# State update and layer-norm sums in two f16 parts; diagonal blocks of keys and state placed by DMA

## The reference

```
x = x + 0.5 * ffn(layernorm(x))
x = x + attn(layernorm(x))
x = x + 0.5 * ffn(layernorm(x))

ffn:  h = silu(x W1 * s1) * (x W2 * s2);  h = gelu(h H1 * t1);  h = gelu(h H2 * t2);  h W3 * s3
      (1024 hidden features, all weights in {-1, 0, 1})
attn: q, k, v, beta = split(layernorm(x) Wqkvb + b);  beta = sigmoid(beta);  k = k / |k| per head
      for every token t, per head (16 heads of 16 features):
          S = S + outer(beta_t * (v_t - S k_t), k_t);   o_t = S q_t
      x + o Wout + b
```

## Time and profile before

| | |
|---|---|
| median of 3 executions | 1703.59 us |
| profiled execution, own time | 1703.29 us |
| its span, first to last instruction | 1701.5 us |
| granted TensorE clock, mean | 0.998 |
| busy: PE / PEld | 97% / 60% |
| busy: DVE / ACT / POOL | 74% / 74% / 75% |

### The profile page before, as it was taken

The page is one execution under the profiler, slowest core; times in us unless marked ns, Lnnn a source line. Parts: engine busy times, 40 slices in busy tenths (PEclk is TensorE's granted clock), DMA queues, the critical chain, the costliest instruction groups (busy, mean ns, idle before and its releaser), DMA issues.

```text
span 1701.5 us, 31307 instructions
## 1 busy us (share of the span) xinstructions
PE 1651.6 (97%) x10385; PEld 1016.2 (60%) x10385; DVE 1258.3 (74%) x3152; ACT 1251.0 (74%) x2510; POOL 1279.5 (75%) x1594
## 2 busy tenths in 40 slices
PE   6989999999999999999999999999999999999999
PEld 5765556565656555565656565555656565655578
DVE  5456787878788787878787887878787878878541
ACT  4668687777778686887777786867877777867654
POOL 4574887969686877869696868778696868687563
PEclk9999999999999999999999999999999999999999
DMA  7200000000000000000000000000000000000000
GB/s 279 75 1 1 1 2 1 2 1 1 1 26 1 1 1 1 26 1 2 1 26 1 2 1 1 1 1 26 1 1 1 2 1 14 1 3 12 13 2 13
DMA packets 5279, 23.26 MB, mean 14 GB/s; under 512 B 640, under 2 KB 1664, under 8 KB 3584
## 3 DMA queue, kind: packets, MB, share of 16 engines
q1 hardware_dynamic: 5120, 21.26, 3.4%
HBM read 17.06 MB, written 4.19 MB: 12 GB/s over the span
## 4 chain that ended last, share of the span: by engine, by line
PE 60%; DVE 12%; POOL 8%; ACT 6%; issue 5%; DVEq 0%; POOLq 0%; ACTq 0%
PE ffn_bank L1152 37%; PE att_bank L1173 6%; PE ffn_bank L1135 5%; PE state_bank L1211 3%; POOL hid_lo L600 3%; POOL pairs L629 2%; DVE terms L998 2%; PE att_bank L1188 2%; PE att_bank L1189 2%; PE att_bank L1220 2%; ACT state_parts L783 2%; PE att_bank L1103 2%; DVE state_bank L1000 2%; DVE roots L875 1%; POOL pairs_lo L637 1%
## 5 line engine op out<-in xcount | busy, mean ns | idle before, releaser
L1152 PE MATMUL ffn_bank<-hid_hi,w_sb 128*128 128x448 f16 (+1 forms) x2880 | 941.0, 337 | 7.6 <-ACT hid L732 3.8
L1152 PE MATMUL ffn_bank<-hid_lo,w_sb 128*128 128x448 f16 (+1 forms) x2880 | 940.9, 337 | 0.0
L600 POOL TENSOR_TENSOR hid_lo<-hid,hid_hi 128x448 f16<-128x448 f32 (+1 forms) x480 | 466.2, 989 | 180.8 <-ACT hid_hi L708 180.6
L1152 PEld LDWEIGHTS ffn_bank<-hid_hi,w_sb 128*128 128x128 fp8e4 x2880 | 285.6, 99 | 210.6 <-issue 10.8
L1152 PEld LDWEIGHTS ffn_bank<-hid_lo,w_sb 128*128 128x128 fp8e4 x2880 | 282.1, 98 | 209.2 <-issue 14.7
L629 POOL TENSOR_TENSOR pairs<-KQ 128x288 f32<-128x288 f32 (+15 forms) x496 | 319.9, 667 | 108.2 <-DVE KQ L925 105.5
L637 POOL TENSOR_TENSOR pairs_lo<-pairs,pairs_hi 128x448 f16<-128x448 f32 (+15 forms) x416 | 319.7, 784 | 31.5 <-ACT pairs_hi L797 31.5
L708 ACT CAST hid_hi<-hid 128x448 f16<-128x448 f32 (+1 forms) x480 | 240.1, 537 | 35.7 <-DVE hid L897 32.9
L732 ACT ACTIVATE hid<-ffn_bank,par_sb 128x448 f32<-128x448 f32 (+1 forms) x320 | 175.6, 600 | 110.9 <-PE ffn_bank L1152 103.9
L797 ACT CAST pairs_hi<-pairs 128x448 f16<-128x448 f32 (+15 forms) x416 | 168.6, 439 | 81.4 <-POOL pairs L629 76.2
L1135 PE MATMUL ffn_bank<-xn_hi,w_sb 128*128 128x448 f16 (+1 forms) x640 | 211.7, 340 | 16.2 <-DVE hid L897 9.0
(11 more groups left out here) (95 smaller groups left out, 2220.7 us busy)
## 6 DMA issues: line engine op xcount, KB each, us to landing
NK<-in_w SPq DMA_DIRECT2D x11, 1024.0 KB, 5.9
X<-in_x SPq DMA_DIRECT2D x7, 512.0 KB, 3.7
out<-X SPq DMA_DIRECT2D x7, 512.0 KB, 2.6
wqkvb_sb<-in_wqkvb SPq DMA_DIRECT2D x1, 1024.0 KB, 8.5
X<-in_x SPq DMA_DIRECT2D x2, 256.0 KB, 6.5
out<-X SPq DMA_DIRECT2D x2, 256.0 KB, 2.1
wout_sb<-in_wout SPq DMA_DIRECT2D x1, 256.0 KB, 9.6
par_sb<-in_par SPq DMA_DIRECT2D x1, 24.0 KB, 2.5
```

The costliest lines, as they stand in the source:

```text
L600: pool.tensor_tensor(hid_lo[layer % 2][:, m, 0:call.width], hid[:, u % HID_BUFFERS, 0:call.width], hid_hi[layer % 2][:, m, 0:call.width], ...
L1152: mm = nc.tensor.matmul(ffn_ps(call, j), weight(name, kk, 2 * pair + i), v[:, kk, cols], start=kk == 0 and part == 0, stop=kk == KT_FF - 1 ...
```

## The change

1. The state update is taken in f16. Keys and u are split in a high and a low part (`KTr`, `Kz` and the new `Uz_parts` are f16 with two parts), and each of the 4 float32 matmuls becomes 4 f16 ones, high and low of the keys with high and low of u: 16 matmuls of 64 columns a chunk. The keys come from the parts that already exist (`KQ_parts`), through one transpose of twice the elements. For u, ScalarE makes the high part (`high_u`) and GpSimd the low part (`low_u`) behind VectorE's transpose.
2. The layer-norm sums are split in the same way (ScalarE `sum_high`, `sq_high`; GpSimd `sum_low`, `sq_low`), and mean and variance are two f16 matmuls each, for all norms but the first.
3. The diagonal blocks of `Kz` and of `state_parts` are placed by DMAs from SP's queue, four of 32 rows each time, in place of ScalarE's copies. The stores and loads of x are put in order among them.
4. The low part of the normed x goes from GpSimd to VectorE.
5. The tables of ticks are changed throughout, and the head of the program mixes weight conversion and the first products in another order.

```diff
-E_RETR = [2, 22, 43, 66]
-E_STATE = [16, 37, 58, 83]
+E_RETR = [2, 23, 46, 66]
+E_STATE = [17, 40, 59, 82]
...
-SPLIT_LAG, SPREAD_LAG = 1, 4
+SPLIT_LAG, SPREAD_LAG = 1, 3
...
+TURN_LEAD, U_HIGH_LEAD, U_LOW_LEAD = 5, 3, 1
...
-        KTr = sb("KTr", [P, 2, GP, 32])
-        Kz = sb("Kz", [P, GP, P])
+        KTr = sb("KTr", [P, 2, 2, GP, 32], F16)
+        Kz = sb("Kz", [P, 2, GP, P], F16)
         Uz = sb("Uz", [P, GP, 2, 32])
+        Uz_parts = sb("Uz_parts", [P, 2, GP, 64], F16)
...
+            def make_kz(w, c):
+                i = w * HCH + c
+                if i:
+                    sp.wait_ge(dstate_ready, i)
+                sp.wait_ge(k_turned, i + 1)
+                for q in range(QUADS):
+                    rows = slice(q * 32, (q + 1) * 32)
+                    sp.dma_start(Kz[rows, :, :, q * 32:(q + 1) * 32], KTr[rows, c % 2, :, :, :]).then_inc(kz_ready, 16)
+
+            def spread_state(w, c):
+                i = w * HCH + c
+                sp.wait_ge(state_lo_ready, 2 * i + 2)
+                for q in range(QUADS):
+                    rows = slice(q * 32, (q + 1) * 32)
+                    sp.dma_start(state_parts[rows, :, :, rows], own_parts[rows, :, :, :]).then_inc(state_ready, 16)
...
+                if part == "sum_low" and i:
+                    pool.wait_ge(sum_hi_ready, i)
+                    pool.tensor_tensor(sum_parts[:, 1, 0:n], feature_sum[:, cols], sum_parts[:, 0, 0:n], ALU.subtract).then_inc(sum_lo_ready, 1)
...
+            def low_u(w, c):
+                i = w * HCH + c
+                pool.wait_ge(u_hi_ready, i + 1)
+                pool.tensor_tensor(Uz_parts[:, 1, :, :], Uz[:, :, :, :].rearrange("p g b w -> p g (b w)"), Uz_parts[:, 0, :, :], ALU.subtract).then_inc(u_ready, 1)
...
+                if part == "sum_high" and i:
+                    act.wait_ge(ln_summed, i + 1)
+                    act.copy(sum_parts[:, 0, 0:n], feature_sum[:, cols]).then_inc(sum_hi_ready, 1)
...
+            def high_u(w, c):
...
+                act.wait_ge(u_turned, i + 1)
+                act.copy(Uz_parts[:, 0, :, :], Uz[:, :, :, :].rearrange("p g b w -> p g (b w)")).then_inc(u_hi_ready, 1)
...
+                if part == "low" and job.kind != "att":
+                    dve.wait_ge(ln_hi, job.n + 1)
+                    nc.vector.tensor_tensor(xn_lo[:, :, cols], xn[:, :, cols], xn_hi[:, :, cols], ALU.subtract).then_inc(ln_lo, 1)
...
-                nc.vector.transpose(KTr[:, c % 2, :, :].rearrange("p g w -> p (g w)"), KQ[:, 0, chunk * GB * C:(chunk + 1) * GB * C]).then_inc(k_turned, 1)
+                nc.vector.transpose(KTr[:, c % 2, :, :, :].rearrange("p a g w -> p (a g w)"),
+                                    KQ_parts[:, :, 0, chunk * GB * C:(chunk + 1) * GB * C]).then_inc(k_turned, 1)
...
+                        nc.tensor.matmul(ps[:, 0:n], average16[:, :], sum_parts[:, 0, 0:n], start=True, stop=False)
+                        nc.tensor.matmul(ps[:, 0:n], average16[:, :], sum_parts[:, 1, 0:n], start=False, stop=True).then_inc(att_filled, 1)
...
                 for g in range(GP):
-                    mm = nc.tensor.matmul(state_ps[:, g * 64:(g + 1) * 64], Kz[:, g, :], Uz[:, g, :, :].rearrange("p b w -> p (b w)"),
-                                          start=False, stop=True, skip_group_check=True)
+                    for k_part in range(2):
+                        for u_part in range(2):
+                            mm = nc.tensor.matmul(state_ps[:, g * 64:(g + 1) * 64], Kz[:, k_part, g, :], Uz_parts[:, u_part, g, :],
+                                                  start=False, stop=True, skip_group_check=True)
```

More of the change, by code:

```diff
@@ L561, in ln @@
                 i, cols = job.i, job.cols
-                total = feature_sum[:, cols].unsqueeze(1)
+                total, n = feature_sum[:, cols].unsqueeze(1), cols.stop - cols.start
                 if part == "sum":
@@ L683, in ln @@
                 n = cols.stop - cols.start
+                if part == "sum_high" and i:
+                    act.wait_ge(ln_summed, i + 1)
+                    act.copy(sum_parts[:, 0, 0:n], feature_sum[:, cols]).then_inc(sum_hi_ready, 1)
+                if part == "sq_high" and i:
+                    act.wait_ge(ln_sq_summed, i + 1)
+                    act.copy(sum_parts[:, 0, 0:n], feature_sum[:, cols]).then_inc(sq_hi_ready, 1)
                 if part == "square":
@@ L757, in key_root @@
                 act.activation(k_sq[:, :], bank_of("norm", w, 0)[:, :], ACT.Sqrt).then_inc(att_read_s, 1)
[L759 to L763, removed]
-                act.wait_ge(k_turned, i + 1)
-                for q in range(QUADS):
-                    rows = slice(q * 32, (q + 1) * 32)
-                    act.copy(Kz[rows, :, q * 32:(q + 1) * 32], KTr[rows, c % 2, :, :]).then_inc(kz_ready, 1)
             def save_q(w, c):
@@ L776, in save_q @@
                 act.copy(O_low[:, c * GB * C:(c + 1) * GB * C].rearrange("p (g t) -> p g t", t=C), queries[:, :, :, 1]).then_inc(att_read_s, 1)
-            def spread_state(w, c):
+            def high_u(w, c):
                 i = w * HCH + c
-                act.wait_ge(state_lo_ready, 2 * i + 2)
-                for q in range(QUADS):
-                    rows = slice(q * 32, (q + 1) * 32)
-                    act.copy(state_parts[rows, :, :, rows], own_parts[rows, :, :, :]).then_inc(state_ready, 1)
+                if i:
+                    act.wait_ge(dstate_ready, i)
+                act.wait_ge(u_turned, i + 1)
+                act.copy(Uz_parts[:, 0, :, :], Uz[:, :, :, :].rearrange("p g b w -> p g (b w)")).then_inc(u_hi_ready, 1)
             def high_kq(w):
@@ L1004, in turn_u @@
                 dve.wait_ge(solve_step, (i + 1) * STEPS * 2)
[L1005 removed]
+                nc.vector.transpose(Uz[:, :, :, :], gapped()).then_inc(u_turned, 1)
             def split_state(w, c):
@@ L1064, in alone @@
                 if job:
-                    for part in ("center", "recip", "norm"):
-                        ln(part, job)
-                if second:
-                    for i in range(2):
-                        convert(i)
-                    for i in range(2, 2 + KT_FF // 2):
-                        mix(call, 2 * i - 4)
-                        mix(call, 2 * i - 3)
-                        convert(i)
+                    ln("center", job)
+                    convert(0)
+                    ln("recip", job)
+                    ln("norm", job)
+                    ln("low", job)
+                if second:
+                    convert(1)
+                    for m in range(KT_FF):
+                        mix(call, m)
+                        if m in HEAD_CONVERTS:
+                            convert(2 + HEAD_CONVERTS.index(m))
+                    convert(4)
+                    convert(5)
                     ln("center", second)
@@ L1078, in alone @@
                     ln("norm", second)
+                    ln("low", second)
                     for i in range(W_PIECES - 2, W_PIECES):
```

109 lines of the change are left out of this document (69 added, 40 removed).

## The result

The changed kernel takes 1769.9 us (median of four executions, 1765.96 to 1773.36) against 1703.0 us: 1.039 times as long, 95% interval 1.037 to 1.042. The forecast was 1662 us, faster, with a range of 1652 to 1706; it came out 66.9 us slower than the kernel before, and above the range. The profiled execution took 1765.96 us, its span is 1764.2.

A forecast was written before the change was run, and what follows sets the result against it. TensorE's queue, busy 97% of the span, was taken as the bound. From 1703.3 us, 46.0 came off (26.2 update, 11.8 and 8.0 norm sums) and 5 were added for DMA stalls: 1662 us, range 1652 to 1706.

The forecast's parts named there:

- State update: Update as 16 f16 matmuls instead of four float32: 0.47 us for 0.88, saving 26.2 us over 64 chunks.
- time taken out of TensorE's queue comes off the end one for one, until another wait opens: Bounding step: TensorE, busy 97% of the span, is full, so its queue is what is paid; 46.0 us come off.
- Norm sums: Layer-norm sums as two f16 steps instead of one float32 sum: 11.8 us (448 columns) and 8.0 us (256) saved.
- State blocks: Four DMAs between update and retrieval: fourth lands 3.1 us after the split, stalling 0.3 us x 16 frames = 5 us.
- The sentence that named over 4 us as a sign of being wrong: Sign: the prediction is wrong if the four state-block DMAs land over 4 us behind VectorE's split.
- Outside TensorE's queue these edits cost nothing by themselves: Other engines: ScalarE lighter, GpSimd 80% to some 86%, VectorE 80% to 84%; none becomes the bound, no cost.
- The longer way to the update: u goes VectorE, ScalarE, GpSimd, TensorE, with 1.4 to 2.2 us to spare: counted as hidden, nothing either way.
- rival B: Less gain: u's low part comes late over three queues, TensorE stands 0.4 us a chunk, 26 us back: 1688 us; chance 0.15.
- Rival A: Slower: 64-byte DMA packets cost 48 ns like large ones, near 1828 us; sign: state_parts waits over 40 us; chance 0.17.
- Rival C: Slower: small f16 matmuls bound by their weights, 0.11 us each, an update 1.76 us: 1744 us; chance 0.02.
- The range: 1652 to 1706 us: takes in rival B and rival A's mild part, leaves out its heavy part and rival C.

The follow-up runs named there:

- e8: e5 with the state update in float32 again (keys and u unsplit, keys' blocks still by DMA): 1706.0 us, ratio 1.0017 to the kernel before.
- e14: e13 with the state update in f16 parts, u split over ScalarE and GpSimd: 1689.9 us, ratio 0.9918 to the kernel before.
- e7: e5 with each norm sum as one float32 matmul again, without high and low parts: 1725.3 us, ratio 1.0132 to the kernel before.
- e5: Changed kernel; GpSimd waits until the norm's product is done, one place later than in e4, behind u's last low part: 1712.1 us, ratio 1.0049.
- e13: e12 plus the second stand: GpSimd also waits until the attention norm's product is done, behind two pairs_lo: 1683.7 us, ratio 0.9883.
- e4: Changed kernel with one wait added: GpSimd stands at the norm's tick until VectorE's product of the norm is done: 1714.7 us, ratio 1.0074.
- e12: e8 with two of the four state DMAs issued by ScalarE's queue, two by SP's: 1705.7 us, ratio 0.9984, ten executions from 1687.5 to 1714.1.

## Why the prediction was wrong, by its own steps

- **State update, 26.2 us:** the step is as sized (0.47 us, 624.10 to 624.57), and so is what left TensorE's queue in all (about 50 us, by busy time and clock, against 46.0). But "time taken out of TensorE's queue comes off the end one for one, until another wait opens" was used without the second half. e8 and e14 show the waits that opened at once: net +6 us each.
- **Norm sums, 19.8 us:** e7 gives 13. The steps are as sized (0.39 us for 448 columns, 0.22 for 256). The split sums make TensorE wait for roots, in the kernel after 17.3 + 2.6 + 2.5 = 22.4 us against 4.9 before (L631 is the low part of the squares' sum); in e7, with float32 sums, it is 3.2 us. But in e7 other waits grew ("issue" 13.3 to 27.4, NK 1.1 to 8.4), so the waits for roots can't simply be set against the 20 us.
- **State blocks, 5 us for a landing at 3.1:** mis-sized. It is 4.0: issues 0.66 us apart and not 0.47, and 2.0 us from issue to landing. The sentence that named over 4 us as a sign of being wrong was met, barely: the retrieval starts 4.1 us behind the split's end (627.30 to 631.41). TensorE waits 30.8 us for these DMAs, not 5. The Trainium skill (DMA: Bandwidth & Descriptors, section "Anatomy of one DMA — SWDGE (gpsimd) path") puts the fixed part at about 2.0 us, and states it for DMAs that GpSimd issues. For these, issued by SP, the rows agree with it and not with the 1.3 us that I took from a store. e5 to e14, and e8 to e13, each give 22 us for two queues and the second stand together; in e5 and e8 the product that the second stand frees took 0.8 us already, so most of the 22 should be the price of one queue.
- **"Outside TensorE's queue these edits cost nothing by themselves":** this is the step that failed. It priced VectorE by its load (80 to 84% of the steady part) and took the 1680 ns product of the earlier trace rows for the instruction's own time. With GpSimd standing it takes 1081 (e4). In the row of before 600 ns were already time held behind GpSimd. With the queues in another order 600 ns became 3.7 us, ahead of the split that TensorE waits for. e4 and e5 put it at 55 to 58 us of the 108 between 1662 and 1770, clock included. The clock itself stood in no term of the sum: it was taken as 1.00 throughout.
- **The longer way to the update:** hidden in the kernel after, as said (waits for u 1.4 us in all), so rival B in its stated form was wrong. Its mechanism, a low part that comes late through ScalarE and GpSimd, is there for the norm sums instead, where I hadn't looked.
- **Rival A** foresaw the right wait for the wrong reason: it is above 40 us in all for L1271, but a group with half the packets (`Kz`, 16 KB) lands after 1.9 us and one of 32 KB after 2.0, so packets of 64 bytes aren't dear (16 more of them to an engine cost about 0.1 us). **Rival C** is refuted by 0.47 us.
- **The range** had no case for an operation off the path that gets several times longer.

Adding up from 1662: +58 for the held product (e5), +22 for the second queue with the second stand (e14), and 28 left in e14, whose trace shows 17 us more wait for roots than before, 16 for the blocks and 5 for hid_lo; waits for u and hid, 15 us before, fell to 6.

## What to carry to other kernels

A change that only shortens the full engine's queue moves the loop that feeds it onto the path: price that loop to the landing of its last transfer before counting the gain. Read one form's durations over all its occurrences before using their mean, and set them against another form of the same operation; where they differ with equal operands, or by more than their sizes do, a part of each is time held by another engine, and another order can multiply it. Where VectorE stands behind a long unbroken run of GpSimd, one semaphore wait in GpSimd's queue can be worth more than all the work removed.

In the kernel before this could be seen. Of the product of 896 elements 15 of 16 took 1.69 to 1.72 us, so its own spread hid the hold. But the product of 512 elements, by form, is 1254 ns in the mean; 14 of the 20 took 1.5 us and the other six 0.65 to 0.69:

```profile
L884 DVE TENSOR_TENSOR xn<-xc,roots 128x512 f32<-128x512 f32 x20 | 25.1, 1254 | 0.1
```

## What the runs showed of the hardware

- VectorE's product of two SBUF tensors can be held to the end of GpSimd's run of instructions (4.79 us where 1.08 are its own; 6.27 at most in e12), or only to the end of one of them (1.70 us in the kernel before, with the next GpSimd instruction held in turn). Once GpSimd waits on a semaphore it gets in (1.08 in e4). At one and the same offset either of them may win (e12). Why GpSimd lets VectorE in between two instructions in the one case and not in the other stays open; e13 only makes the question idle.
- A DMA between two SBUF tensors in 32 rows of 64-byte pieces takes SP 0.66 us to issue and 2.0 us to land. Two queues issue side by side: the fourth landed 2.97 us behind the first issue in e13 (510.05 to 513.02), where one queue takes 4.0 (the kernel after and e8). The Trainium skill (DMA: Bandwidth & Descriptors, section "Rules for kernel authors") says that spreading DMAs over queues saves issue time and no more; the runs agree, and here issue time was what counted.
- 16 f16 matmuls of 64 columns, each with weights of its own, go by in 0.47 us, 29 ns each; the four float32 ones of the update take 0.84 us in e8 and e13.
